# A two-layer transformer block on eight cores: batched statistics and stores, one set of scratch buffers, and weight halves loaded over two queues

## The reference

```python
x = x + LN(attn0(LN(x)))      # causal attention, one head of width 1024
x = x + LN(ffn0(LN(x)))
x = x + LN(attn1(LN(x)))      # trilinear attention over the last 32 tokens, then W_O, + input, LN
x = x + LN(ffn1(LN(x)))

def ffn(x):                   # hidden width 3072, integer weights scaled by 1/127
    h = silu(x @ wg.T) * (x @ wu.T)
    return h @ wd.T
```

## Time and profile before

| what | us |
|---|---|
| time, median of 2 runs | 5082.89 (5077.7 to 5088.07) |
| the profiled execution's own time | 5094.35 |
| its span, slowest core (core 3) | 5092.8 |
| spans of the 8 cores | 5029.6 to 5092.8 |
| TensorE matmul busy | 3137.9 (62%) |
| VectorE, ScalarE, GpSimd busy | 1143.8, 978.0, 273.7 |

### The profile page before, as it was taken

One profiled execution on the slowest core, in us unless ns is written; L12 is line 12 of the kernel. 1 busy time (PEld: TensorE's weight loads), 2 busy tenths in 40 slices (PEclk: granted clock), 3 DMA queues, 4 the chain that ended last, 5 costly groups with the idle time before them and its releaser, 6 DMA issues.

```text
span 5092.8 us, 41456 instructions; the slowest of 8 cores (5029.6 to 5092.8 us)
## 1 busy us (share of the span) xinstructions
PE 3137.9 (62%) x14368; PEld 1377.7 (27%) x14368; DVE 1143.8 (22%) x2314; ACT 978.0 (19%) x1695; POOL 273.7 (5%) x192
## 2 busy tenths in 40 slices
PE   2800266668858641396757576666897952088967
PEld 1300122233323210142323232223342311033423
DVE  1000112131113335411112101213111444521112
ACT  1400132131100023311100333213110012321100
POOL 0000000000001100000012000000000100000012
PEclk9855577679878855698979787767998965589988
DMA  9999500042343114005252300001203121002041
GB/s 171 108 110 109 61 1 1 3 109 59 102 93 131 42 45 96 0 38 124 67 161 81 93 17 1 1 0 62 82 31 124 50 83 50 0 25 75 38 153 75
DMA packets 238333, 340.03 MB, mean 67 GB/s; under 512 B 205936, under 2 KB 206064, under 8 KB 224944
## 3 DMA queue, kind: packets, MB, share of 16 engines
q0 software_dynamic: 13120, 165.68, 15.4%
q1 hardware_dynamic: 224192, 169.90, 13.4%
q10 hardware_dynamic: 816, 1.80, 0.1%
HBM read 236.68 MB, written 159.38 MB: 78 GB/s over the span
## 4 chain that ended last, share of the span: by engine, by line
PE 56%; DMA 13%; DVE 9%; ACT 8%; another core or an unknown queue 6%; issue 5%; SPq 2%; DVEq 0%; ACTq 0%; POOL 0%; POOLq 0%
PE PSA L690 25%; PE PSA L772 14%; PE PSA L582 5%; PE PSA L443 3%; PE PSA L495 3%; PE PSA L517 2%; DMA A<-s_wq 2%; ACT A L343 2%; DMA hs<-A 2%; PE PST L338 2%; PE PSA L459 2%; DMA A<-s_d 1%; SPq L401 1%; DMA A<-s_g 1%
## 5 line engine op out<-in xcount | busy, mean ns | idle before, releaser
L690 PE MATMUL PSA<-A 128*128 128x512 bf16 x6144 | 1350.9, 383 | 150.1 <-DMA A<-s_g 86.0
L772 PE MATMUL PSA<-A 128*128 128x512 bf16 x3072 | 705.6, 394 | 273.2 <-DMA A<-s_d 148.9
L690 PEld LDWEIGHTS PSA<-A 128*128 128x128 bf16 x6144 | 603.9, 99 | 895.6 <-issue 188.5
L703 DVE SCALAR_TENSOR_TENSOR A<-PSA,FA 128x512 bf16<-128x512 f32 x384 | 263.7, 691 | 1282.0 <-PE PSA L690 1179.9
L338 PE MATMUL PST<-IDN,A 128*128 128x128 bf16 x768 | 94.8, 301 | 700.0 <-ACT A L632 433.4
L772 PEld LDWEIGHTS PSA<-A 128*128 128x128 bf16 x3072 | 307.8, 101 | 671.0 <-issue 334.5
L698 ACT ACTIVATE FA<-PSA 128x512 f32<-128x512 f32 x384 | 229.3, 597 | 1248.7 <-PE PSA L690 1248.6
L582 PE MATMUL PSA<-A 128*128 128x512 bf16 x544 | 252.4, 562 | 161.1 <-ACT A L573 74.0
L495 PE MATMUL PSA<-A 128*128 128x512 bf16 x512 | 128.0, 417 | 350.4 <-DMA A<-s_wq 341.8
L338 PEld LDWEIGHTS PST<-IDN,A 128*128 128x128 bf16 x768 | 72.4, 135 | 724.8 <-issue 724.8
L805 POOL TENSOR_TENSOR X<-FA,X 128x1024 f32<-128x1024 f32 x64 | 150.0, 2343 | 635.5 <-DVE FA L800 635.5
(11 more groups left out here) (146 smaller groups left out, 2276.3 us busy)
## 6 DMA issues: line engine op xcount, KB each, us to landing
hs<-A POOLq DMA_DIRECT2D x32, 1536.0 KB, 5.6
A<-hs SPq DMA_DIRECT2D x32, 1536.0 KB, 9.6
X<-x_in SPq DMA_DIRECT2D x32, 512.0 KB, 19.2
out<-X POOLq DMA_DIRECT2D x32, 512.0 KB, 5.4
s_g<-g POOLq DMA_DIRECT2D x2, 6144.0 KB, 213.2
s_u<-u POOLq DMA_DIRECT2D x2, 6144.0 KB, 271.2
s_d<-d POOLq DMA_DIRECT2D x2, 6144.0 KB, 327.8
wgt<-A POOLq DMA_DIRECT2D x4, 3072.0 KB, 10.8
```

The costliest lines, as they stand in the source:

```text
L690: p.op("tensor", lambda e, lhs=lhs, rhs=rhs, pp=pp, cc=cc: e.matmul(PSA[:, pp * 1024: pp * 1024 + 512], lhs, rhs, start=(cc == 0), stop=(c ...
L703: p.op("vector", lambda e, pu=pu, d=hdst, sgo=sgo: e.scalar_tensor_tensor(out=d, in0=PSA[:, pu * 1024: pu * 1024 + 512], scalar=DQ, in1=FA ...
L772: p.op("tensor", lambda e, lhs=lhs, rhs=rhs, pp=pp, dh=dh, hc=hc: e.matmul(PSA[:, pp * 1024 + dh * 512: pp * 1024 + (dh + 1) * 512], lhs, ...
```

## The change

Four edits, of which three undo a refinement and one adds one:

1. For `s == 1`, `ffn_whalf_load` splits each of the two weight loads into halves of 6144 columns (1.57 MB): first the two first halves from SP, in the slots used before, then the two second halves from POOL, in slots `wdg` and `wdg2`.
2. The second pass uses FT0, BN1 and the columns TB 4 to 10 for every tile, where it took two sets by turns.
3. The statistics for attention 1 are taken for all four groups after the last group of the second pass.
4. The 16 stores of `out` are issued after the last group of layer 1.

```diff
@@ ffn_whalf_load, s == 1
-                    p.dma("sync", ... out=A[:, FWGH:FWGH + 12288], in_=wgt[layer][...],
-                        r=[("wgt", layer, half)], w=AK(FWGH, 12288), slot=slg)
-                    p.dma("sync", ... out=A[:, FWUH:FWUH + 12288], in_=wut[layer][...],
-                        r=[("wut", layer, half)], w=AK(FWUH, 12288), slot=slu)
+                    for q in range(2):
+                        eng_ = "sync" if q == 0 else "gpsimd"
+                        p.dma(eng_, lambda e, layer=layer, half=half, q=q: e.dma_start(
+                            out=A[:, FWGH + q * 6144:FWGH + (q + 1) * 6144],
+                            in_=wgt[layer][:, half * 12288 + q * 6144: half * 12288 + (q + 1) * 6144]),
+                            r=[("wgt", layer, half)],
+                            w=AK(FWGH + q * 6144, 6144),
+                            slot=(slg if q == 0 else "wdg"))
+                        p.dma(eng_, lambda e, layer=layer, half=half, q=q: e.dma_start(
+                            out=A[:, FWUH + q * 6144:FWUH + (q + 1) * 6144],
+                            in_=wut[layer][:, half * 12288 + q * 6144: half * 12288 + (q + 1) * 6144]),
+                            r=[("wut", layer, half)],
+                            w=AK(FWUH + q * 6144, 6144),
+                            slot=(slu if q == 0 else "wdg2"))
@@ ffn_layer2, second pass
-                        FTd = FT0 if tsub % 2 == 0 else FT1
-                        tbb_ = 4 if tsub % 2 == 0 else 12
-                        bnn = BN1 if tsub % 2 == 0 else BN2
-                        bnk = ("bn", tsub % 2)
...
-                        p.op("vector", lambda e, pp=pp, b=tbb_, FTd=FTd: e.tensor_scalar(
-                            out=FA[:, FTd:FTd + 1024], in0=PSA[:, pp * 1024: pp * 1024 + 1024],
+                        p.op("vector", lambda e, pp=pp: e.tensor_scalar(
+                            out=FA[:, FT0:FT0 + 1024], in0=PSA[:, pp * 1024: pp * 1024 + 1024],
...
-                    if post_group is not None:
-                        post_group(g)
-
-            def l1a_stats_group(g_):
+
+            ffn_layer2(0)
+
+            for g_ in range(4):
                 tiles = [4 * g_ + tt for tt in range(4)]
                 ln_stats_batch2(
...
-            ffn_layer2(0, post_group=l1a_stats_group)
...
-            def store_group(g_):
-                for t in range(4 * g_, 4 * g_ + 4):
-                    dst = out[xoff + t * 128: xoff + (t + 1) * 128, :]
...
-            ffn_layer2(1, prep_done=True, post_group=store_group)
+            ffn_layer2(1, prep_done=True)
+
+            for t in range(16):
+                dst = out[xoff + t * 128: xoff + (t + 1) * 128, :]
+                p.dma("gpsimd", lambda e, t=t, dst=dst: e.dma_start(
+                    out=dst, in_=X[:, t * 1024:(t + 1) * 1024]),
+                    r=[("x", t)], slot="out")
```

More of the change, by code:

```diff
@@ L668, in ffn_whalf_load @@
                 else:
-                    p.dma("sync", lambda e, layer=layer, half=half: e.dma_start(
-                        out=A[:, FWGH:FWGH + 12288],
-                        in_=wgt[layer][:, half * 12288:(half + 1) * 12288]),
-                        r=[("wgt", layer, half)], w=AK(FWGH, 12288), slot=slg)
-                    p.dma("sync", lambda e, layer=layer, half=half: e.dma_start(
-                        out=A[:, FWUH:FWUH + 12288],
-                        in_=wut[layer][:, half * 12288:(half + 1) * 12288]),
-                        r=[("wut", layer, half)], w=AK(FWUH, 12288), slot=slu)
+                    for q in range(2):
[12 more added lines that the diff above has]
+                            slot=(slu if q == 0 else "wdg2"))
             def ffn_pass1_group(layer, half, g):
@@ L712, in ffn_pass1_group, with ffn_layer2 @@
                               r=AK(hbase, 6144), w=[("hs", g, half)], slot="ho")
-            def ffn_layer2(layer, prep_done=False, half0_done=False,
-                           post_group=None):
+            def ffn_layer2(layer, prep_done=False, half0_done=False):
                 sdp = s_ffn["d%d" % layer]
@@ L794, in ffn_layer2 @@
[L794 to L799, removed]
-                        p.op("vector", lambda e, pp=pp, b=tbb_, FTd=FTd: e.tensor_scalar(
-                            out=FA[:, FTd:FTd + 1024], in0=PSA[:, pp * 1024: pp * 1024 + 1024],
-                            scalar1=TB[:, b:b + 1], scalar2=TB[:, b + 6:b + 7],
+                        p.op("vector", lambda e, pp=pp: e.bn_stats(
+                            BN1[:, 0:6], PSA[:, pp * 1024: pp * 1024 + 512]),
+                            r=PK(2 * pp), w=[("bn", 0)])
@@ new lines, in ffn_layer2 @@
+                        p.op("vector", lambda e, pp=pp: e.bn_stats(
+                            BN1[:, 6:12], PSA[:, pp * 1024 + 512: pp * 1024 + 1024]),
+                            r=PK(2 * pp + 1), w=[("bn", 0)])
+                        p.op("vector", lambda e: e.bn_aggr(TB[:, 4:6], BN1),
+                             r=[("bn", 0)], w=TK(4, 2))
+                        p.op("vector", lambda e: e.tensor_scalar(
+                            out=TB[:, 7:8], in0=TB[:, 5:6], scalar1=DQ * DQ,
+                            scalar2=EPS_LN, op0=ALU.mult, op1=ALU.add),
+                            r=TK(5), w=TK(7))
@@ new lines, in ffn_layer2 @@
+                        p.op("scalar", lambda e: e.activation(
+                            out=TB[:, 8:9], in_=TB[:, 7:8], func=AF.Ln),
+                            r=TK(7), w=TK(8))
+                        p.op("scalar", lambda e: e.activation(
+                            out=TB[:, 9:10], in_=TB[:, 8:9], func=AF.Exp, scale=-0.5),
+                            r=TK(8), w=TK(9))
+                        p.op("vector", lambda e: e.tensor_scalar(
+                            out=TB[:, 10:11], in0=TB[:, 9:10], scalar1=DQ,
+                            scalar2=None, op0=ALU.mult), r=TK(9), w=TK(10))
@@ L803, in ffn_layer2 @@
+                        p.op("vector", lambda e, pp=pp: e.tensor_scalar(
+                            out=FA[:, FT0:FT0 + 1024], in0=PSA[:, pp * 1024: pp * 1024 + 1024],
+                            scalar1=TB[:, 4:5], scalar2=TB[:, 10:11],
                             op0=ALU.subtract, op1=ALU.mult),
-                            r=PK(2 * pp, 2) + TK(tbb_) + TK(tbb_ + 6), w=FK(FTd, 1024))
-                        p.op("gpsimd", lambda e, t=t, FTd=FTd: e.tensor_tensor(
+                            r=PK(2 * pp, 2) + TK(4) + TK(10), w=FK(FT0, 1024))
@@ L806, in ffn_layer2 @@
+                        p.op("gpsimd", lambda e, t=t: e.tensor_tensor(
                             out=X[:, t * 1024:(t + 1) * 1024],
-                            in0=FA[:, FTd:FTd + 1024],
+                            in0=FA[:, FT0:FT0 + 1024],
                             in1=X[:, t * 1024:(t + 1) * 1024], op=ALU.add),
-                            r=FK(FTd, 1024) + [("x", t)], w=[("x", t)])
-                    if post_group is not None:
-                        post_group(g)
-            def l1a_stats_group(g_):
+                            r=FK(FT0, 1024) + [("x", t)], w=[("x", t)])
```

17 lines of the change are left out of this document (removed).

## The result

The changed kernel takes 1.0148 of the time before, 95% interval 1.0128 to 1.0167: 75 us more (65 to 85), about 5158 us. Its profiled execution took 5163.39 us by its own time, against 5094.35 before. The forecast was 5153, with 5133 to 5181 around it.

What follows compares the result with a forecast made beforehand. No engine was full (PE 56% of the chain of waits, DMA 13%), so the change counted at the seams: 26.6 + 22.5 + 32.7 - 3.6 - 8 = +70.2 us, giving 5153 on the median of the runs, range 5133 to 5181.

Steps and rivals of the forecast that it cites:

- statistics, sequence 0: Ahead of attention 1: three groups of 8.87 us now precede group 3, delaying the first projection's load by 26.6 us.
- statistics, sequence 1: Ahead of attention 1: PE starts 26.6 us later, but a shorter third-projection load wait leaves +22.5 us.
- stores at the seam, at the end: After layer 1's last group, between sequences and at program end: 12 more stores remain, 16.3 us each time at 385 GB/s.
- one scratch set: Second pass: normalisation must wait for POOL's last addition, but has 6.5 us of slack, so nothing is lost.
- second halves, two layers: Sequence 1's gate and up loads: weights land no sooner, PE lacks four matmuls instead of eight, -1.8 us per layer.
- quarters, two layers: Second pass, down weights: quarter 3 follows quarter 2, `hs` of group 1 waits behind; last quarter 4 us sooner per layer.
- The rival of a sinking burst: The 16 stores put out at once slow down, deciding from 15.8 us more per seam; slower by over 2%; chance 0.13.
- Rival B: Two queues bring bandwidth, the serial quarter costs little: -5.4 and -6.2, each twice; +58.6 in all, 5141; chance 0.12.
- C: POOL's queue makes weights late: +3 us per half load, nothing gained at the quarters; +87.8 in all, 5171; chance 0.10.
- D: Ahead of attention 1, the statistics hide: a load wait or DVE's cadence gives back, say, half; 5128; chance 0.05.

Runs made afterwards that it cites:

- e5: The changed kernel with the four groups of statistics behind the second pass in the order 3, 0, 1, 2; ratio 1.0153 to the kernel before.
- e4: The kernel before with only one scratch set for every tile of the second pass; ratio 1.0022 to the kernel before.
- e6: The changed kernel with its 16 stores issued by SP instead of POOL, each waiting for its own tile only; ratio 1.0086 to the kernel before.

## Why the prediction was right

The time lay 5 us above the forecast. Step by step, with the means of the eight cores in the traces:

| term | predicted | measured |
|---|---|---|
| statistics, sequence 0 | +26.6 | +26.3 at the copy; +27.3 at the fourth projection's load |
| statistics, sequence 1 | +22.5 | +26.3 at PE's start; +21.5 at the same load |
| stores at the seam, at the end | +16.3, +16.3 | +17.6, +17.8 |
| one scratch set | 0 | pace the same |
| second halves, two layers | -1.8, -1.8 | -0.4 each, lost in a spread of 8 and more |
| quarters, two layers | -4, -4 | -1.1, -1.1 |
| sum | +70.2 | about +81 (+75 by the ratio, 65 to 85) |

- The statistics came out as worked, both the 26.6 and the 4 us that sequence 1 gets back (4.8). The reason given held half the truth. The prediction laid the wait on DVE's own order; ACT's list holds line 821 just as firmly, and with DVE's order put right (e5) not a microsecond came back.
- The stores cost 2.7 us more than forecast. The rate of a single 6.29 MB store with rows of 48 KB, 385 GB/s, was taken for a burst of small ones; the 12 more of them took 17.6 and 17.8 us, which is 357 and 353 GB/s. The Trainium skill (HBM Reference, Specifications) gives about 358 GB/s per core of a pair, and the 17.6 us per seam estimated from it lay nearer than the 16.3 taken. The rows do not show it as a ceiling: single stretches of the burst ran at up to 412 GB/s, though with the cores up to 17 us apart no row tells whether the other core of the pair was storing then. The rival of a sinking burst is out: the slowest stretch of any core, at 313, is far from the 196 from which it decides.
- The scratch set costs nothing. The pace of e4 is the pace of before.
- The halves bring nothing that can be seen. From the gate load of half 1 to the first `h` store behind it, it is 68.86 us on the profiled core of both kernels (3669.37 to 3738.23, and 3703.95 to 3772.81). Over all cores and both layers the mean is 67.8 us in the five kernels that do not split (65.0 to 71.3) and 67.5 in the nine that do (62.7 to 73.0); from the kernel before to the changed one it even rises, from 66.8 to 67.4. The 1.8 us that four matmuls instead of eight should give are smaller than this spread and neither shown nor ruled out. Rival B's bandwidth isn't there: in the 24 us of this load the split kernel has a DMA share of 0.92 at 310 GB/s, the unsplit one 0.93 at 328.
- The quarters had the right order of events and the wrong size. The forecast read both its figures from one core, the slowest, where POOL's issue of quarter 2 comes 19.7 us ahead of the last quarter's first matmul; the mean of the eight is 18.3 and 18.0 in the two layers (15.5 to 21.2). After the change it is 16.8 and 16.3, near the 15.7 that the forecast worked out. So the step itself gains 1.5 and 1.7 us and not 4. The other half of the term, from the `hs` load to POOL's issue, was taken as unchanged; it is 17.2 and 16.6 before, 17.6 and 17.2 after, though SP now sends quarter 0 0.9 us behind `hs` (3910.20) where it was 8.9 (3881.28). Sent so early, it shares the engines with `hs`: up to POOL's issue the profiled cores moved 5.4 MB at 298 GB/s before and 5.5 MB at 285 after, so the earlier start gained nothing.
- Of the other rivals, C (weights 3 us late per half load, nothing gained at the quarters) is not there in full, but at the quarters the truth, -1.1, lies nearer to it than to the forecast's -4. D (the statistics hide) fell by the copy's 26.3 us.

All four misses of size (stores 2.7, halves 2.8, quarters 5.8, statistics -0.3) come to +11 us, those of stores, halves and quarters within the bounds that the prediction gave them, and the time moved by 5 only. The seams' +81 lies inside the ratio's interval, so nothing contradicts, but that the forecast came so near is in part luck. What stays open is the 0.3% between the sum of the four edits alone and the whole, and e6's 47 us by the seams against 31 by the ratio, both within the intervals or at their edge.

## What to carry to other kernels

Work moved behind a loop costs its full duration when the next stage's first instruction stands behind it in any one engine's list: look up every list, since putting one of two right gave nothing and putting both right gave back all but some 2 us. Stores that an engine issues wait for whatever stands before them in its list, so issue them where nothing does: from SP, behind the last group, they left 6.6 us from the last normalisation to the next load, where the kernel before needed 11.4 (means of the eight cores) with POOL's stores after every group. And size a term by several cores: read off the slowest one alone the quarters promised 4 us, and the mean of eight gave 1.1. And where a seam is set by loads that go one by one, ask first why they are eight.

## What the runs showed of the hardware

- Sixteen stores of 512 KB in a burst ran at 360 to 373 GB/s from GpSimd on the profiled core, in stretches of 4 us at 313 to 412 over all eight cores, and at 353, 406 and 382 in successive stretches from SP on its profiled core; a single store of 6.29 MB had 385.
- Eight transfers of 256 KB, each waiting for the one before, took 2.5 to 3.3 us apiece, 19.5 us from the first issue to the last. One transfer of 2 MB took 8.7 to 10.9 from issue to landing.
- Splitting a weight load over two queues left the DMA share at 0.92 and the rate no higher. The rule of the Trainium skill (DMA: Bandwidth & Descriptors, Rules for kernel authors), that spreading over issuing engines brings no bandwidth, agrees with these rows.
